# Mixture stages of a fused attention, expert and scan kernel: tiles of gathered tokens transposed through DRAM and VectorE instead of TensorE

## The reference

```python
x = x + attention(layernorm(x))
x = x + mixture(layernorm(x))
x = x + scan(layernorm(x))
x = x + mixture(layernorm(x))

def mixture(x):                       # E = 8 experts, 2 chosen per token, I = 938
    out = swiglu(x, shared_gate_up, shared_down)
    cw = weights of the two best experts of each token, normalised, 0 elsewhere
    for e in range(8):
        out = out + cw[..., e:e+1] * swiglu(x, gate_up[e], down[e])
    return out
# swiglu(x, gu, d): g, u = split(x @ gu.T); (silu(g) * u) @ d.T
```

## Time and profile before

| | |
|---|---|
| median of 3 runs | 2079.09 us (2078.61 to 2080.23) |
| profiled execution, own time | 2079.64 us |
| profiled execution, span | 2077.9 us |
| TensorE busy | 2004.4 us, 96% of the span |
| VectorE, ScalarE, GpSimd busy | 1447.2, 1205.6, 1441.6 us |
| granted TensorE clock | 0.994 over the span |

### The profile page before, as it was taken

The page is one execution under the profiler, slowest core; times in us unless marked ns, Lnnn a source line. Parts: engine busy times, 40 slices in busy tenths (PEclk is TensorE's granted clock), DMA queues, the critical chain, the costliest instruction groups (busy, mean ns, idle before and its releaser), DMA issues. The chain is left out here.

```text
span 2077.9 us, 43374 instructions
## 1 busy us (share of the span) xinstructions
PE 2004.4 (96%) x14806; PEld 1569.0 (76%) x14807; DVE 1447.2 (70%) x2668; ACT 1205.6 (58%) x2403; POOL 1441.6 (69%) x989
## 2 busy tenths in 40 slices
PE   7999999999999999999999999999799999999998
PEld 5886448999999646666666666766664499999994
DVE  6887684333333589999999999999987733333335
ACT  5776423222222269999999999999853232222222
POOL 6884005767777439999999999999930077777760
PEclk9999999999999999999999999999999999999999
DMA  8000100000001433343433333333342000000014
GB/s 315 2 2 12 31 1 20 25 25 25 24 24 27 120 110 104 113 115 112 110 114 118 113 114 104 116 111 114 102 188 100 3 25 25 25 25 24 25 24 125
DMA packets 94725, 151.37 MB, mean 73 GB/s; under 512 B 27612, under 2 KB 61790, under 8 KB 92423
## 3 DMA queue, kind: packets, MB, share of 16 engines
q1 hardware_dynamic: 85510, 131.10, 20.5%
q0 software_dynamic: 9088, 18.63, 3.2%
HBM read 132.52 MB, written 17.24 MB: 72 GB/s over the span
## 5 line engine op out<-in xcount | busy, mean ns | idle before, releaser
L2458 POOL TENSOR_TENSOR m_seen<-m_state,experts 128x1024 f32<-128x1024 f32 (+1 forms) x256 | 598.4, 2368 | 12.7 <-DVE m_state L2513 10.7
L2513 DVE TENSOR_TENSOR_SCAN m_state<-experts,ps 128x512 f32<-128x512 f32 x448 | 537.5, 1234 | 1.8 <-issue 1.1
L1986 PE MATMUL ps<-ident,m_seen 128*128 128x128 f32 x2040 | 270.6, 276 | 23.8 <-POOL m_seen L2458 23.7
L2250 ACT ACTIVATE experts<-delta,experts 128x512 f32<-128x512 f32 x448 | 291.3, 712 | 0.5 <-DVE delta L2535 0.2
L1986 PEld LDWEIGHTS ps<-ident,m_seen 128*128 128x128 f32 x2040 | 234.8, 142 | 63.1 <-POOL m_seen L2458 45.0
L1644 POOL COPY f_weights<-experts 128x1898 f32 x142 | 251.8, 1773 | 22.9 <-issue 20.7
L1465 PE MATMUL ps<-zu,f_weights 128*128 128x128 f32 x1988 | 241.4, 275 | 0.3 <-issue 0.3
L1465 PE MATMUL first_up_ps<-f_xT,f_weights 128*128 128x128 f32 x1988 | 241.4, 275 | 0.3 <-issue 0.3
L1465 PEld LDWEIGHTS ps<-zu,f_weights 128*128 128x128 f32 x1988 | 233.2, 192 | 1.0 <-issue 1.0
L1465 PEld LDWEIGHTS first_up_ps<-f_xT,f_weights 128*128 128x128 f32 x1988 | 233.2, 192 | 1.0 <-issue 1.0
L1632 POOL DMA_INDIRECT f_xin<-tokens,f_take x71 | 69.7, 981 | 215.0 <-DVE f_take L1160 133.0
(11 more groups left out here) (485 smaller groups left out, 3963.0 us busy)
## 6 DMA issues: line engine op xcount, KB each, us to landing
experts<-m_rows SPq DMA_DIRECT2D x144, 512.0 KB, 3.7
experts<-in_experts SPq DMA_DIRECT2D x17, 1461.0 KB, 18.0
tokens<-f_rows SPq DMA_DIRECT2D x8, 512.0 KB, 4.6
f_rows<-expert_out SPq DMA_DIRECT2D x8, 512.0 KB, 7.0
f_cols<-expert_out SPq DMA_DIRECT2D x8, 512.0 KB, 7.2
experts<-m_diagonal SPq DMA_DIRECT2D x16, 256.0 KB, 4.0
counting<-m_diagonal SPq DMA_DIRECT2D x16, 256.0 KB, 4.4
out<-X SPq DMA_DIRECT2D x4, 512.0 KB, 3.2
```

The lines of the kernel that those rows point to most:

```text
L1986: mm = pe.matmul(Y[:, i // 2, at:at + P], seen[:, n % SEEN, h, i * P:(i + 1) * P], ident[:], is_transpose=True, start=(n == 0 and at == 0) ...
L2250: act.activation(PB[n % B_RING][:, h, :] if n in AWAY else dA[:, n % DECAYS, h, :], delta[:, U % 2, h, :], ACT.Exp, scale=decay[:, lhn:lhn ...
L2458: pool.tensor_tensor(seen[:, n % SEEN, :, part], state[:, n % RING, :, part], row.unsqueeze(1).to_broadcast([P, HALF, row.shape[-1]]), ALU ...
L2513: dve.tensor_tensor_scan(state[:, n % RING, h, :], decay_, drive_, before_, ALU.mult, ALU.add).then_inc(s_state, 1)
```

## The change

In both mixture stages, the tiles of slots 2 to 70 are no longer transposed by TensorE. The gathered tile is stored to DRAM (`laid_out`, four buffers), by ScalarE behind its first silu of the body two slots ahead (by SyncE for slots 2 and 3). SyncE then loads it back into `xT` with four DMAs, one for each group of 32 partitions, which put the 32x32 block (i, j) in the place of block (j, i). VectorE then transposes the 16 blocks where they stand, with one instruction. Slots 0 and 1 go the old way. ScalarE's copy from PSUM is left out for slots 2 to 70. VectorE's body begins with the index copy for slot t + 3 and the transpose of slot t + 1; the index copy for slot 2 moves into the shared expert's part. The buffer `xin` comes free by the store (`s_xout`), not by TensorE.

```diff
@@ names and the store
+BLOCK = 32
+BLOCKS = P // BLOCK
+TURNED_FIRST = 2
+        laid_out = [nc.dram_tensor(f"laid_out_{n}", (UNROLL, P, D), F32, kind="Internal").ap() for n in range(2)]
+                    def lay_out(eng, s, k):
+
+                        eng.dma_start(laid_out[n][k], xin[:, s, :]).then_inc(s_xout[s], 16)
@@ VectorE
+                                    elif k == MARKED_AT[BATCHES] + 2:
+                                        dve.wait_ge(s_xin[0], 16)
+                                        dve.tensor_copy(take[:, 0:1], source[:, 2:3]).then_inc(s_take, 1)
...
-                            dve.wait_ge(s_xin[0], 16)
-                            dve.tensor_copy(take[:, 0:1], source[:, 2:3]).then_inc(s_take, 1)
+                            def turn_blocks(t, s):
+
+                                dve.wait_ge(s_blocks, (t + 1 - TURNED_FIRST) * 16 * BLOCKS)
+                                dve.transpose(xT[:, s, :], xT[:, s, :]).then_inc(s_xT2, 1)
 
                             def body(t, s, i):
                                 if exists(t):
-                                    dve.wait_ge(s_gA, t + 1)
-                                    dve.tensor_tensor(hT[:, s, A], gated[:, A], UP_A, ALU.mult).then_inc(s_hA, 1)
                                     if exists(t + 3):
                                         dve.wait_ge(s_xin[1 - s], (t + s) * 8 + 16)
                                         dve.tensor_copy(take[:, 1 - s:2 - s], source[:, ds(t + 3, 1)]).then_inc(s_take, 1)
+                                    if exists(t + 1) and not (isinstance(t, int) and t + 1 < TURNED_FIRST):
+                                        turn_blocks(t + 1, 1 - s)
+                                    dve.wait_ge(s_gA, t + 1)
+                                    dve.tensor_tensor(hT[:, s, A], gated[:, A], UP_A, ALU.mult).then_inc(s_hA, 1)
@@ ScalarE
-                                    if exists(t + 1):
+                                    if exists(t + 2) and not (isinstance(t, int) and t < TURNED_FIRST):
+                                        act.wait_ge(s_xin[s], (t - s) * 8 + 32)
+                                        lay_out(act, s, (i + 2) % UNROLL)
+                                    if isinstance(t, int) and t + 1 < TURNED_FIRST:
                                         next_columns(t + 1, 1 - s)
@@ SyncE
+                            for t in range(TURNED_FIRST, SLOTS):
+                                s, of = t % 2, t // 2 * 16
+                                if t < 2 * TURNED_FIRST:
+                                    sp.wait_ge(s_xin[s], of + 16)
+                                    lay_out(sp, s, t % UNROLL)
+                                by_block = laid_out[n][t % UNROLL].rearrange("(i b) (j a) -> j b i a", b=BLOCK, a=BLOCK)
+                                sp.wait_ge(s_xout[s], of)
+                                wait(sp, s_blocks, (t - TURNED_FIRST) * 16 * BLOCKS)
+                                sp.wait_ge(s_upB, t - 1)
+                                for j in range(BLOCKS):
+                                    sp.dma_start(xT[j * BLOCK:(j + 1) * BLOCK, s, :].rearrange("b (i a) -> b i a", a=BLOCK), by_block[j]).then_inc(s_blocks, 16)
@@ GpSimd, gather
-                                wait(pool, s_tx, t - 1 if isinstance(t, int) else freed)
+                                if isinstance(t, int) and t < 2 * TURNED_FIRST:
+                                    wait(pool, s_tx, t - 1)
+                                else:
+                                    pool.wait_ge(s_xout[s], (t - s) * 8 - 16 if isinstance(t, int) else freed)
```

More of the change, by code:

```diff
@@ L896, in ffn @@
                     s_written, s_hot, s_inverted, s_take = ts("written"), ts("hot"), ts("inverted"), ts("take")
-                    s_xin, s_tx, s_xT2 = [ts("xin0"), ts("xin1")], ts("tx"), ts("xT")
+                    s_xin, s_home = [ts("xin0"), ts("xin1")], [ts("home0"), ts("home1")]
+                    s_tx, s_xout, s_blocks, s_xT2 = ts("tx"), [ts("xout0"), ts("xout1")], ts("blocks"), ts("xT")
                     s_upA, s_upB, s_gA, s_gB, s_gZ, s_hA, s_hB = (ts(x) for x in ("upA", "upB", "gA", "gB", "gZ", "hA", "hB"))
@@ L903, in ffn @@
                     s_yS, s_tS, s_xS, s_late, s_sum = (ts(x) for x in ("yS", "tS", "xS", "late", "sum"))
-                    s_home, s_g = [ts("home0"), ts("home1")], [ts(f"g{c}") for c in range(QUARTERS)]
+                    s_g = [ts(f"g{c}") for c in range(QUARTERS)]
                     GROUPS = NT // GROUP
@@ L1627, in gather @@
                                 if not isinstance(t, int):
-                                    pool.reg_mov(freed, t - 1)
+                                    pool.reg_mov(freed, (t - s) * 8 - 16)
                                 pool.wait_ge(s_written, 16 * QUARTERS)
                                 pool.wait_ge(s_take, gathered)
-                                wait(pool, s_tx, t - 1 if isinstance(t, int) else freed)
+                                if isinstance(t, int) and t < 2 * TURNED_FIRST:
+                                    wait(pool, s_tx, t - 1)
+                                else:
+                                    pool.wait_ge(s_xout[s], (t - s) * 8 - 16 if isinstance(t, int) else freed)
                                 pool.indirect_dma_start(xin[:, s, :], None, tokens_out[n], bass.IndirectOffsetOnAxis(ap=take[:, s:s + 1].bitcast(U32), axis=0)).then_inc(s_xin[s], 16)
```

## The result

Six runs of each kernel, in turns: 2061.55 us (2059.11 to 2063.22) against 2079.07 us (2077.71 to 2080.23), a ratio of 0.9911 with a 95% interval of 0.9902 to 0.9921. The change makes the kernel faster by 17.5 us by the medians, 18.5 by the ratio. The profiled execution took 2060.88 us, its span is 2059.1, 18.8 us under that of before.

The account below looks back on a forecast made before the run. TensorE, busy throughout the mixture slots, was taken as the bound: 2079.64 us minus 15.3 for 138 transposes, everything added being hidden, gives 2064.3, stated as 2064. Own range 2061 to 2067; for 8 in 10, 2061 to 2079.

Parts of the forecast that it names:

- TensorE's row is the bound: Mixture slots: TensorE busy the whole window; removing 138 transposes at 0.111 us each takes off 15.3 us.
- The exchange is hidden behind two slots: Mixture slots: store, loads, VectorE's transpose and next product end at 9.04 us, before TensorE's need at 10.26; chance 0.70.
- The cover: Mixture slots: spare time between the chain's end at 9.04 us and TensorE's need at 10.26, put at 1.2 us.
- The two-slot rule: Mixture slots: each us of chain past 10.26 costs 0.5 us a slot, since two tiles are under way at once.
- The gather: GpSimd's gather in the slots: starts about 1.1 us sooner with the early index copy, 2.3 us to spare before ScalarE's store.
- The stage's start: First slots of each mixture stage, with slot 2's earlier gather: put at nothing, with 2 us a stage at most.
- The range's lower edge: Whole kernel: 2061 us, the lower end of both the forecast's own range and the 8 in 10 range.
- Short pieces: SyncE's loads in 128-byte pieces: a load at 5.5 us makes slots 6.27 and the kernel slower, 2222 us; chance 0.08.
- Loaded landings: Store and loads in the slots: slow landings make the chain 12.84 us, slots 6.42, the kernel about 2242 us; chance 0.11.

Follow-up runs that it names:

- experiment 3: Kernel before with only the index copies moved earlier, transposes staying on TensorE: 2078.55 us, ratio 0.9993.
- 4: Kernel before with each transpose of slots 2 to 70 done twice on TensorE: 2095.19 us in a single execution.
- experiment 7: Changed kernel with eight loads in place of four and ScalarE's store behind its last silu of the slot: 2231.58 us in a single execution.
- experiment 6: Changed kernel with ScalarE's store behind its last silu of the slot instead of the first: 2075.55 us in a single execution.
- experiment 9: Changed kernel with the index copies of the bodies behind the first product again, slot 2's staying early: 2068.70 us in a single execution.
- experiment 1: The changed kernel run again without an edit: 2065.46 us, ratio 0.9922 against the kernel before.
- experiment 8: Changed kernel with the four loads taking contiguous rows of 512 bytes, exchange of blocks left out: 2067.59 us in a single execution.

## Why the prediction was right or wrong

- **TensorE's row is the bound, and a transpose costs its place in it.** Right, and shown from both sides (experiments 3 and 4): 0.109 us each, 15.1 us for 138, foretold 15.3.
- **The exchange is hidden behind two slots.** Right; the slots are 5.13 us with TensorE busy throughout. The cover was larger than foretold, some 2.5 us in the slot shown and 2.1 at the median (10.26 - 7.12 - 0.31 - 0.69) instead of 1.2: the store starts with the silu, at 2.07 and not at 2.64, and the first product, foretold 0.55 us late, was pushed back in 3 of 68 slots a stage only. The single prices were right: store to load 1.8 (taken 1.8), load to transpose 1.8 (taken 2.0, and 0.2 for the hand-overs), transpose 0.31 (taken 0.29). The two-slot rule, half a microsecond a slot for each over it, is borne out by experiment 7 to 0.3 us a slot; the point from which it decides is shown by 6 to be a matter of the tail of the stores and landings, not of the median.
- **The gather.** Right: it starts 2.6 to 3.0 us into a slot and no longer 4.1, and is not on the path. With the exchange, the early place of its index copy is worth about 2 us (experiment 9); the expectation of that experiment had it as nothing.
- **The stage's start, put at nothing.** This term was wrong: it is 0.55 us a stage, 1.1 in all. The sum looked at when slot 2's gather could go and not at what stands behind that gather in GpSimd's queue, the weights of slot 1, which TensorE was waiting for. With it the sum is 15.1 + 1.1 = 16.2, what the slots in the two traces show.
- **The first stage's end, not in the sum at all.** The prediction looked at the slots and their start. The results' loads come 1.7 us sooner behind the last store in every kernel with the exchange, and VectorE idles some 0.8 us less (experiment 1). The cause stays open. With it the sum is 17.0.
- **The range's lower edge.** This is where the prediction failed, by the terms that it put at nothing: the two above, 1.1 and 0.8 us, and chance. Its edge, 2061, is 2079.64 less 16.6 (0.12 us for each of 138 transposes) and less 2 us for the starts of both stages, though the text allowed 2 us for each. Measured against the runs of before the ratio is 0.9911, or 2060.6 us beside the 2079.09 that was known, just outside; the repeat is 2062.9 by its ratio. The sum of 16.2 gives 2062.9 as well, that of 17.0 gives 2062.1; with either the first six runs also had luck in them. The stretch between the stages takes 962.7 to 968.0 us from one execution to the next, mostly with TensorE's granted clock. The range reached 15 us upward for the rivals and 3 down, and that was too little: the two medians of the changed kernel, 2061.55 and 2065.46, are 3.9 us apart. The transposes, the main term, were right to 0.2 us.
- **The rivals.** Short pieces: refuted by experiment 8 for loads of 16 KB. The Trainium skill (DMA: Bandwidth & Descriptors, Specifications) sets 512 bytes as the least piece for line rate; the time of a 16 KB load did not depend on it, 1.81 against 1.79 us, while its share of the DMA engines did. The Trainium skill (DMA: Bandwidth & Descriptors, Rules for kernel authors) puts a transpose by a rearranged access pattern 19 times behind the hardware's own; no run here compares the two, and the loss that the prediction drew from it as its second rival did not come. The Trainium skill (VectorE: DVE Perf Modes, The three transpose paths) has 311 ns for a bfloat16 tile of 128x128; the trace agrees, with 311 ns for float32. Loaded landings: the medians stayed at 1.8 us. Single ones reached 3.12 us in the changed kernel and were covered; in experiment 6, with 1.7 us less room, landings of up to 2.98 us behind stores up to 1.1 us late were not.

## What to carry to other kernels

Where one engine is busy through a whole window, an instruction taken off it is worth its spacing in the timeline (0.11 us here), not its printed length (0.27), and a detour of 5 us over DRAM is free if it has two slots to run in. Work out the chain from the first to the last link, compare it with the number of slots that the buffers allow, and leave room for the slowest landing rather than for the median one: with 0.3 us of room at the median a third of the slots came out longer (51 of 140), with 2 us none. When an instruction is moved earlier, look at what stands behind it in its queue and behind whatever it releases; that is where one unforeseen microsecond was. And read the stretches that a change is not meant to touch in more than one trace of each kind before they are called chance.

## What the runs showed of the hardware

- A DMA issued by ScalarE's queue behind an activation starts with the activation and not behind it (341.72, the activation from 341.70 to 342.30): 0.02 us after its start at the median, and before its end for 132 of 134 stores of the changed kernel. The store reads another tile than the activation writes.
- Stretches of 3.4 us at half of TensorE's clock appear in the scan stage in some executions and not in others, none to three of them, and each goes with about 1.5 us. That is most of the difference between the twelve traces in the stretch between the stages.
- A gather's wait was put down to TensorE by the trace of before, while it started 0.74 us behind VectorE's index copy in slot after slot; with the index copies early (experiment 3) and nothing else changed, the gathers start 2.84 us into a slot and no longer 4.17. The constant distance, not the named releaser, pointed to the cause.
